# Perceiver layer on one core: three rounded query products, three context buffers, one buffer for residual and output, and new engine orders

## The chip, the core and the metric

The kernel runs on one core of a Trainium2 chip. A core has a matrix engine (TensorE, PE in the profile, with PEld for its weight loads), a vector engine (VectorE, DVE), an activation engine (ScalarE, ACT), a general one (GpSimd, POOL) and SyncE (SP), which here only issues DMAs. Each runs its own instructions in order and they meet at semaphores. The time is that of one execution on the device, in microseconds (us). Before the change it is 835.1 us, the median of three runs from 832.51 to 836.73.

## What is computed

The reference is one perceiver layer over 64 sequences of 32 tokens with 256 channels, each with 257 context rows of 192 channels. Cut to what matters:

```python
x = x + cross_attention(layernorm(x), ctx)     # 16 heads of 64; Wq 256x1024, Wkv 192x2048, Wo 1024x256; key mask
x = x + self_attention(layernorm(x))           # 16 heads of 16, over the 32 tokens of a sequence
r = sigmoid(mix(x, mu_r) @ Wr.T)               # mix: mu * x + (1 - mu) * x of the token before
x = x + r * (square(relu(mix(x, mu_k) @ Wk.T)) @ Wv.T)
```

Both attentions normalise again with a layer norm of their own. All is in fp32, inputs and output.

## The kernel before

The 64 sequences are worked in 8 groups of 8 (GB), so a group has 256 tokens (TOK). The keys of the cross attention are never made: the queries of a group are multiplied with the key weights first (jobs K0 to K11, L677 to L713), which gives for each head a row of 192 numbers to multiply with the context itself.

A long stream of named jobs is written out by hand for each engine: one list for the first group, one for the six middle groups, one for the last group (L63 to L128). A job is called by its name; `:3` behind it is the sequence of the group. The names that matter here:

- CT transposes the context of a sequence (TensorE, L746), rounds it to `cT_h` (ScalarE, L1101) and takes the rest to `cT_l` (VectorE, L1365). S0 to S3 are the scores of a sequence, four heads at a time: five products of 258 columns into one bank (L807), mask and maximum (VectorE, L1374), exponential (ScalarE, L1109). R are reciprocals (VectorE), N the normalising on GpSimd (L565), P the transposes of probabilities (L818, copied at L1117), U their rounding (ScalarE, L1128), L their rest (GpSimd, L431), AC ten products with the context (L835 to L841; 512 columns), whose results ScalarE (L1141, L1142) and VectorE (L1387) copy. CU and CL round the context for AC (L1135, L422 and L423).
- For the group that comes next: A0 to A9 (layer norm, VectorE), XT (transposes of the normalised tokens, L638, copied to `xnT` at L1053), Q0 to Q3 (queries, L657, copied to `qT` at L1057) and K0 to K11 (product L712; rounding on ScalarE L1088, L1092; rest on VectorE L1352, L1356). K0 to K3 and K6, K7 are written into two pairs of banks in turn, so K4 waits for the rests of K0 and K1, and so on. The scores of the next group wait for the rest of K9, those of its last four heads for K11.
- For the group that went before, behind its cross attention: OT0, OT1 (values, L875 to L887), WO0, WO1 (output product, L895, added to the residual at L1411), B0 to B9 (layer norm), T2, QT, KT, VR, SC, PT, PV, T4, PJ (self attention), C0 to C9, T3, M0, M1, FR, FK, KA, FV, YO (feed forward; KA on GpSimd L601, FV at L968 and L1502, YO on GpSimd L607, which adds the residual and makes the output `yo`). XB and X1 (GpSimd, L584, L590) add a bias row to the residual.

What stands after `CT:0` at the end of a list belongs to the next group. In the last group's list the closing jobs have a half behind them (`WO.0`, `WO.1`), since nothing is left beside them; Z jobs are products whose result nobody reads (L997).

SyncE (L502 to L516) loads in each group the tokens of the next but one stage (`xn`), the residual `xb` of the group before (which waits until `yo` of the group before that was made), then a context buffer each time that CL has freed one (`cx_in`, four of them, L512), and stores `yo`. The last residual and the last store have the same form.

The queries are made of fp32 operands:

```python
last = pe.matmul(pre[:, i * TOK:(i + 1) * TOK], wq[:, k, (2 * n + i) * P:(2 * n + i + 1) * P],
                 xnT[:, k, :], start=(k == 0), stop=(k == 1))
```

One such product of a 128x128 block with 256 columns is two matmul records in the profile; a product of operands of type fp32r is one record.

Of the kernel before, what the change touches and what calls it, by code (L numbers as in the profile page):

```python
# [1597 lines left out]
```

## Time and profile before

| | |
|---|---|
| median of 3 runs | 835.1 us (832.51 to 836.73) |
| the profiled execution's own time | 835.41 us |
| its span in the profile | 832.8 us |
| period of a middle group | 98.5 us |
| first group | 0 to about 99 us |
| closing part, behind the last AC | about 779 to 832.8 us |
| TensorE busy | 801.4 us, 96% of the span |
| VectorE, ScalarE, GpSimd busy | 72%, 73%, 50% |
| granted TensorE clock | 1.00 but for one stretch in the closing part |

The span is the time from the first instruction of the program to the last, and the execution's own time holds 2.6 us more around it. A timeline row gives start and length in us, engine, line, operation, output<-inputs, shapes and count, and in brackets the idle time before it with what ended it. The length of a matmul record includes the way through the array, so two following ones overlap: what a product costs is the distance of starts. A period is the stretch from the first scores of one group to those of the next.

### The profile page before, as it was taken

To read this page: it belongs to the slowest core of one execution; us is meant where nothing else is said; L and a number is where in the kernel's file an instruction comes from. 1 tells how busy PE (TensorE), PEld (TensorE's weight loads), DVE (VectorE), ACT (ScalarE), POOL (GpSimd) and SP (SyncE) were. 2 spreads that over 40 slices of the span, in tenths; PEclk is the share of its full clock that TensorE was granted. 3 is DMA by queue.
4 is the path that set the end of the run, shared out by engine and by line. 5 is a ranking of instruction groups with operands and counts; after the bars stand their busy time and mean duration, and the time that the engine had idled before them with its cause. 6 is when DMAs were issued, how large, how long until landed. Compare 5 with 4: busy or idle time off the path is not lost.

```text
span 832.8 us, 20494 instructions
## 1 busy us (share of the span) xinstructions
PE 801.4 (96%) x7497; PEld 665.5 (80%) x7497; DVE 599.3 (72%) x1813; ACT 604.6 (73%) x1439; POOL 417.0 (50%) x664
## 2 busy tenths in 40 slices
PE   9999899998999999998999989999999999999976
PEld 8988688885889778896788868887688977978755
DVE  4865857787587966879577886778668794688376
ACT  3998857887678965789568976789667895778333
POOL 1356445762456624665347534566245672487311
PEclk9999999999999999999999999999999999999999
DMA  8411210111101201012101111011010110100000
GB/s 234 140 32 44 55 26 15 39 27 39 27 15 39 65 1 39 2 40 64 27 15 27 26 52 27 14 39 48 18 27 14 39 52 14 28 14 1 27 2 13
DMA packets 49522, 30.51 MB, mean 37 GB/s; under 512 B 22928, under 2 KB 48336, under 8 KB 49424
## 3 DMA queue, kind: packets, MB, share of 16 engines
q1 hardware_dynamic: 48528, 29.12, 12.9%
q8 instruction: 60, 0.98, 0.5%
q14 instruction: 38, 0.31, 0.1%
q10 hardware_dynamic: 896, 0.10, 0.1%
HBM read 26.85 MB, written 2.10 MB: 35 GB/s over the span
## 4 chain that ended last, share of the span: by engine, by line
PE 79%; DVE 16%; issue 3%; ACT 1%; DMA 0%; POOL 0%; POOLq 0%; ACTq 0%
PE score L807 18%; PE probT L818 6%; PE pre L657 6%; PE post L895 6%; DVE qk_t L1356 5%; DVE qk_l L1352 3%; PE aux L746 3%; PE post L904 3%; PE ac_main L835 3%; PE ac_tail L837 3%; PE ac_main L836 3%; PE ac_tail L841 3%; PE ac_main L840 3%; PE post L875 2%; PE post L881 2%
## 5 line engine op out<-in xcount | busy, mean ns | idle before, releaser
L431 POOL TENSOR_TENSOR prT_l<-prT,prT_h 128x512 fp32r<-128x512 f32 x128 | 165.3, 1292 | 187.0 <-ACT prT_h L1128 186.5
L565 POOL TENSOR_SCALAR pr<-pr,rsum,poison 128x257 f32<-128x257 f32 x256 | 149.4, 594 | 134.8 <-DVE rsum L1380 134.8
L1109 ACT ACTIVATE pr<-sm,nmx 128x257 f32<-128x257 f32 x256 | 129.5, 507 | 61.2 <-DVE nmx L1374 58.1
L1374 DVE CUSTOM_DVE_ANT_0 sm<-score,mbias 128x257 f32<-128x257 f32 x256 | 106.8, 420 | 75.3 <-PE score L807 60.6
L807 PE MATMUL score<-cT_h,qk_h 128*128 128x258 f32 x256 | 89.7, 350 | 7.3 <-DVE qk_t L1356 6.0
L1128 ACT ACTIVATE prT_h<-prT 128x512 fp32r<-128x512 f32 x128 | 80.5, 630 | 20.3 <-PE ac_tail L841 19.1
L1117 ACT ACTIVATE prT<-probT 128x512 f32<-128x512 f32 x128 | 75.6, 591 | 6.7 <-PE probT L818 4.7
L818 PE MATMUL probT<-ident,pr 128*128 128x128 f32 x512 | 79.3, 277 | 0.0
L807 PE MATMUL score<-cT_h,qk_t 128*128 128x258 f32 x256 | 72.8, 284 | 0.0
L807 PE MATMUL score<-cT_h,qk_l 128*128 128x258 f32 x256 | 72.5, 283 | 0.0
L807 PE MATMUL score<-cT_l,qk_h 128*128 128x258 f32 x256 | 72.5, 283 | 0.0
L807 PE MATMUL score<-cT_l,qk_t 128*128 128x258 f32 x256 | 72.3, 282 | 0.0
L1387 DVE TENSOR_TENSOR act_<-ac_tail,act_low 64x256 f32<-64x256 f32 x128 | 52.6, 411 | 26.7 <-ACT act_low L1141 25.5
L818 PEld LDWEIGHTS probT<-ident,pr 128*128 128x128 f32 x512 | 58.5, 141 | 16.1 <-issue 11.5
L807 PEld LDWEIGHTS score<-cT_h,qk_h 128*128 128x128 f32 x256 | 48.4, 189 | 15.1 <-DVE qk_t L1356 8.6
L835 PE MATMUL ac_main<-prT_h,c_hl 128*128 128x512 f32 x128 | 55.6, 434 | 3.2 <-ACT prT_h L1128 2.0
L1365 DVE TENSOR_TENSOR cT_l<-aux,cT_h 128x512 fp32r<-128x512 f32 x64 | 44.1, 688 | 12.7 <-ACT cT_h L1101 12.0
L657 PE MATMUL pre<-xnT,wq 128*128 128x256 f32 x224 | 52.9, 379 | 0.0
L895 PE MATMUL post<-wo,qT 128*128 128x256 f32 x224 | 50.6, 379 | 0.0
L837 PE MATMUL ac_tail<-prT_h,c_hl 128*128 128x512 f32 x128 | 50.4, 394 | 0.0
L836 PE MATMUL ac_main<-prT_h,c_hl 128*128 128x512 f32 x128 | 50.2, 392 | 0.0
L840 PE MATMUL ac_main<-prT_l,c_hl 128*128 128x512 f32 x128 | 50.1, 392 | 0.0
(319 smaller groups left out, 2170.2 us busy)
## 6 DMA issues: line engine op xcount, KB each, us to landing
cx_in<-in_ctx_dram SPq DMA_DIRECT2D x64, 192.0 KB, 2.5
cx_in<-in_ctx_dram SPq DMA_DIRECT2D x64, 64.0 KB, 2.3
xn<-in_x_dram SPq DMA_DIRECT2D x8, 256.0 KB, 2.9
xb<-in_x_dram SPq DMA_DIRECT2D x8, 256.0 KB, 3.0
out_dram<-yo SPq DMA_DIRECT2D x7, 256.0 KB, 2.2
wq<-in_L_xattn_Wq_dram SPq DMA_DIRECT2D x2, 512.0 KB, 6.0
wo<-in_L_xattn_Wo_dram SPq DMA_DIRECT2D x1, 1024.0 KB, 8.2
wqkv<-in_L_attn_W_qkv_dram SPq DMA_DIRECT2D x1, 768.0 KB, 8.9
```

What stands on the lines that cost most here:

```text
L431: eng.tensor_tensor(prT_l[:, :, cut], prT[:, :, cut], prT_h[:, :, cut], ALU.subtract).then_inc(prob_lower, 1)
L565: last = pool.tensor_scalar(p, p, rsum[:, j % 2, t:t + 1], poison[:, 0:1], ALU.mult, ALU.mult)
L657: last = pe.matmul(pre[:, i * TOK:(i + 1) * TOK], wq[:, k, (2 * n + i) * P:(2 * n + i + 1) * P], xnT[:, k, :], start=(k == 0), stop=(k == 1))
L807: last = pe.matmul(score[t % 2][:, 0:NK + 1], q[:, j, tile], c, start=(i == 0), stop=(i == len(products) - 1))
L818: last = pe.transpose(probT[:, m * 256 + i * P:m * 256 + (i + 1) * P], pr[j % 2][:, 2 * half + i, m * P:(m + 1) * P], ident[:])
L835: pe.matmul(ac_main[:], c[:, m, UPPER], prT_h[:, m, :], start=(m == 0), stop=False)
L837: pe.matmul(ac_tail[:], c[:, m, TAILS], prT_h[:, m, :], start=(m == 0), stop=False)
L895: last = pe.matmul(bank[:, 0:DM], qT[:, k, w * P:(w + 1) * P], wo[:, k, :], start=(k == 0), stop=(k == NPAIR - 1))
L1109: act.activation(pr[j % 2][:, t, :], sm[:, t % 2, :], ACT.Exp, bias=nmx[:, j % 2, t:t + 1], scale=-1.0, accum_out=ssum[:, j % 2, t:t + 1]) ...
L1117: act.activation(prT[:, :, half * 256:(half + 1) * 256], probT[:].rearrange("p (m c) -> p m c", m=2), ACT.Copy).then_inc(probT_copied, 1)
L1128: act.activation(prT_h[:, :, cut], prT[:, :, cut], ACT.Copy).then_inc(prob_upper, 1)
L1374: dve.tensor_tensor_reduce(sm[:, t % 2, :], score[t % 2][:, 0:NK], mbias[:], DH ** -0.5, BIG, ALU.add, ALU.min, nmx[:, j % 2, t:t + 1]).th ...
```

## The change

- The queries of groups 1 to 7 (Q0 to Q3) are made of three rounded products in place of one in fp32: upper weights by upper tokens, lower weights by upper tokens, upper weights by lower tokens, each for two halves of the channels. The first group's queries stay in fp32 (`first_queries`).
- For it `wq` is split once: ScalarE rounds it to `wq_h` in four pieces (jobs V0 to V3), GpSimd takes the rest to `wq_l` (V0 to V3). The tokens are split in each group: ScalarE rounds `xnT` to `xnT_h` right behind the copy XT, GpSimd makes `xnT_l` (XL).
- The fp32 `wq` moves into the second half of `acm`'s storage, so the first `acm` copy waits for the split.
- The context has three loading buffers instead of four; buffer numbers run through all sequences.
- `xb`, `x1`, `x2` and `yo` are one buffer. The residual of a group is loaded once the output of the group before has been stored; X1 waits for the layer norm B9 that reads x1; YO works in place.
- All orders are new, and the closing part has 20 Z products instead of 17. The second half's closing tiles lie in `acm` instead of `wq`.

The diff, cut (of the order lists two lines each of TensorE's and GpSimd's middle ones):

```diff
-NCTX = 4
+NCTX = 3
 PE_ORDER = (
-    "S0:0 CT:1 S1:0 OT0 CT:2 S2:0 S3:0 OT1 LV0 P0:0 S0:1 S1:1 LV1 WO0 S2:1 P1:0 S3:1 WO1 S0:2 XT CT:3 S1:2 P0:1 S2:2 S3:2 "
+    "S0:0 S1:0 CT:1 OT0 CT:2 S2:0 S3:0 OT1 LV0 P0:0 LV1 S0:1 S1:1 WO0 S2:1 CT:3 P1:0 S3:1 WO1 P0:1 S0:2 AC:0 S1:2 S2:2 T2 "
...
-    "S1:7 S2:7 FR S3:7 P0:6 FK AC:5 P1:6 FV K0 K2 P0:7 AC:6 K4 K6 P1:7 LT K8 AC:7 CT:0 K10").split()
+    "FR S2:7 S3:7 FK P0:6 AC:5 FV K0 P1:6 K2 P0:7 LT K4 P1:7 AC:6 CT:0 K6 K8 AC:7 K10").split()
...
-        wq = sb("wq", [P, 2, NH * DH])
+        wq_h = sb("wq_h", [P, 2, NH * DH], F32R)
+        wq_l = sb("wq_l", [P, 2, NH * DH], F32R)
+        xnT_h = sb("xnT_h", [P, 2, TOK], F32R)
+        xnT_l = sb("xnT_l", [P, 2, TOK], F32R)
-        x2 = x1
+        x2 = xb = yo = x1
+        wq = stage[:, 2048:4096].rearrange("p (k n) -> p k n", k=2)
...
             def load_residual(g):
-                after(sp, y_ready, g)
+                if g == 0:
+                    sp.wait_ge(ffn_full, 1)
+                after(sp, stored, 16 * g)
...
-                    load_ctx(g * GB + j + NCTX, j % NCTX)
+                    load_ctx(g * GB + j + NCTX, (g * GB + j) % NCTX)
...
                 elif base == "X1":
-                    pool.wait_ge(*copied("WO1" if a is None else name.replace("X1", "WO"), g))
+                    pool.wait_ge(ln_ready[3] if a == 1 else ln_ready[1], 1 if a == 1 else g + 1)
...
+            def weights_lower(n):
+                pool.wait_ge(wq_upper, n + 1)
+                cut = slice(n * 256, (n + 1) * 256)
+                pool.tensor_tensor(wq_l[:, :, cut], wq[:, :, cut], wq_h[:, :, cut], ALU.subtract).then_inc(wq_split, 1)
+            def tokens_lower(g):
+                pool.wait_ge(xnT_upper, g)
+                pool.tensor_tensor(xnT_l[:], xnT[:], xnT_h[:], ALU.subtract).then_inc(xnT_split, 1)
...
                     n = int(name[1])
+                    if n == 0:
+                        pe.wait_ge(xnT_split, g)
+                    if g == 1:
+                        pe.wait_ge(wq_split, n + 1)
                     for i in range(2):
-                        for k in range(2):
-                            last = pe.matmul(pre[:, i * TOK:(i + 1) * TOK], wq[:, k, (2 * n + i) * P:(2 * n + i + 1) * P],
-                                             xnT[:, k, :], start=(k == 0), stop=(k == 1))
+                        cols = slice((2 * n + i) * P, (2 * n + i + 1) * P)
+                        products = [(w[:, k, cols], t[:, k, :]) for w, t in ((wq_h, xnT_h), (wq_l, xnT_h), (wq_h, xnT_l)) for k in range(2)]
+                        for m, (w, t) in enumerate(products):
+                            last = pe.matmul(pre[:, i * TOK:(i + 1) * TOK], w, t, start=(m == 0), stop=(m == len(products) - 1))
...
                 if name == "XT":
+                    after(act, xnT_split, g - 1)
...
+                    if g > 0:
+                        last.then_inc(pre_free, 1)
+                        act.wait_ge(pre_free, nth_pre("XT", g))
+                        act.activation(xnT_h[:].rearrange("p k t -> p (k t)"), xnT[:].rearrange("p k t -> p (k t)"), ACT.Copy).then_inc(xnT_upper, 1)
+                        return
...
+            def weights_upper(n):
+                act.wait_ge(pre_full, nth_pre("G1", 0))
+                cut = slice(n * 256, (n + 1) * 256)
+                act.activation(wq_h[:, :, cut], wq[:, :, cut], ACT.Copy).then_inc(wq_upper, 1)
```

Below are three places of the new order, each before and after. Lines are numbered anew in the changed kernel.

First, TensorE where the first query job (Q0) of a middle group stands. Before (L657 is Q0, L638 is T2, L904 is QT):

```order
L841 MATMUL ac_tail<-prT_l,c_hl 128x512
L638 MATMUL post<-ident,hn 128x128 x4
L657 MATMUL pre<-xnT,wq 128x256 x4
L904 MATMUL post<-hT,wqkv 128x256 x4
L807 MATMUL score<-cT_h,qk_h 128x258
```

Now (L682 is Q0):

```order
L832 MATMUL score<-cT_l,qk_t 128x258
L682 MATMUL pre<-xnT_h,wq_h 128x256 x2
L682 MATMUL pre<-xnT_h,wq_l 128x256 x2
L682 MATMUL pre<-xnT_l,wq_h 128x256 x2
L682 MATMUL pre<-xnT_h,wq_h 128x256 x2
L682 MATMUL pre<-xnT_h,wq_l 128x256 x2
L682 MATMUL pre<-xnT_l,wq_h 128x256 x2
L832 MATMUL score<-cT_h,qk_h 128x258
```

Q0's four fp32 products are twelve rounded ones, and it stands between two score jobs; the transposes XT stand shortly before it, behind VR, where there was a longer stretch between XT and Q0.

Second, ScalarE at the end of a period, from the copy P0:7 to the rounding of K8 and K9. Before (L1117 P, L1128 U, L1141 and L1142 AC:6, L1088 and L1092 the roundings of K4 to K9):

```order
L1117 ACTIVATE prT<-probT 128x2x256
L1141 ACTIVATE act_low<-ac_tail 64x512
L1142 ACTIVATE acm<-ac_main 128x16x32
L1088 ACTIVATE qk_h<-score 128x8x2x32 x2
L1128 ACTIVATE prT_h<-prT 128x2x256
L1088 ACTIVATE qk_h<-pre 128x8x2x32
L1117 ACTIVATE prT<-probT 128x2x256
L1088 ACTIVATE qk_h<-post 128x8x2x32
L1128 ACTIVATE prT_h<-prT 128x2x256
L1092 ACTIVATE qk_t<-score 64x8x2x32 x4
```

Now (L1148 P, L1159 U, L1174 and L1175 AC:6, L1119 and L1123 the roundings, L1132 the context copy CT:0):

```order
L1148 ACTIVATE prT<-probT 128x2x256
L1159 ACTIVATE prT_h<-prT 128x2x256
L1123 ACTIVATE qk_t<-post 64x8x2x32 x2
L1119 ACTIVATE qk_h<-score 128x8x2x32 x2
L1148 ACTIVATE prT<-probT 128x2x256
L1159 ACTIVATE prT_h<-prT 128x2x256 x2
L1174 ACTIVATE act_low<-ac_tail 64x512
L1175 ACTIVATE acm<-ac_main 128x16x32
L1119 ACTIVATE qk_h<-pre 128x8x2x32
L1119 ACTIVATE qk_h<-post 128x8x2x32
L1132 ACTIVATE cT_h<-aux 128x2x256
L1123 ACTIVATE qk_t<-score 64x8x2x32 x4
```

The rounding of K3 has moved behind the copy P0:7 and U1:6, both roundings U0:7 and U1:7 stand ahead of AC:6, and CT:0 ahead of K8; K0, K1 and K2 stand ahead of this piece, with P1:6 between K1 and K2, where P1:6 and U1:6 stood ahead of K0 before.

Third, GpSimd where the token rest XL was put in, in a middle group (L570 is N, L434 is L, L553 and L554 are the columns of CT, L624 is XL):

```order
L434 TENSOR_TENSOR prT_l<-prT,prT_h 128x2x256
L553 COPY cT_h<-left_h 128x2
L554 COPY cT_l<-left_l 128x2
L570 TENSOR_SCALAR pr<-pr,rsum,poison 128x257 x2
L578 COPY lastp<-pr 128x4
L624 TENSOR_TENSOR xnT_l<-xnT,xnT_h 128x512
L570 TENSOR_SCALAR pr<-pr,rsum,poison 128x257 x2
L434 TENSOR_TENSOR prT_l<-prT,prT_h 128x2x256 x2
```

XL stands between N1:2 and N0:3. And GpSimd at the end of a period, before (L607 is YO, L584 XB of the period that follows):

```order
L607 TENSOR_TENSOR yo<-sc,x 128x512
L565 TENSOR_SCALAR pr<-pr,rsum,poison 128x257 x2
L573 COPY lastp<-pr 128x4
L431 TENSOR_TENSOR prT_l<-prT,prT_h 128x2x256 x2
L548 COPY cT_h<-left_h 128x2
L549 COPY cT_l<-left_l 128x2
L565 TENSOR_SCALAR pr<-pr,rsum,poison 128x257 x2
L548 COPY cT_h<-left_h 128x2
```

Now (L564 is LX, L611 YO, L589 XB):

```order
L434 TENSOR_TENSOR prT_l<-prT,prT_h 128x2x256
L564 TENSOR_TENSOR lv<-lvc,keep 128x512
L434 TENSOR_TENSOR prT_l<-prT,prT_h 128x2x256
L611 TENSOR_TENSOR x<-sc,x 128x512
L434 TENSOR_TENSOR prT_l<-prT,prT_h 128x2x256
L553 COPY cT_h<-left_h 128x2
L554 COPY cT_l<-left_l 128x2
L589 TENSOR_TENSOR x<-x,bo_row 128x256 x2
L553 COPY cT_h<-left_h 128x2
```

YO stands between L0:7 and L1:7 instead of ahead of N1:7, LX has moved in from the next period's start, and XB is the first of the next period.

## Rows read from the trace of the kernel before

**Rows 1.** The page's engine totals.

```profile
PE 801.4 (96%) x7497; PEld 665.5 (80%) x7497; DVE 599.3 (72%) x1813; ACT 604.6 (73%) x1439; POOL 417.0 (50%) x664
```

**Rows 2.** Busy time by stretch, a period's length from the middle, and the closing part.

```profile
core 0: us, PE busy (x) PEld busy (x) DVE busy (x) ACT busy (x) POOL busy (x), PEclk, DMA share, GB/s
...
494.80:593.00 98.20, 95.68 (x890) 79.39 (x889) 73.24 (x220) 74.40 (x174) 51.82 (x81) 1.00 0.11 31
...
776.00:833.00 57.00, 45.91 (x516) 35.07 (x508) 33.19 (x93) 16.44 (x44) 8.86 (x11) 0.93 0.03 10
```

**Rows 3.** Waits of TensorE: waited for, us in total, times, longest.

```profile
PE score L807 <- DVE qk_t L1356: 6.0, 6, 1.0
PE pre L712 <- DVE qk_t L1356: 3.1, 7, 0.5
PE score L712 <- DVE qk_l L1352: 3.0, 7, 0.6
PE ac_main L835 <- ACT prT_h L1128: 2.0, 6, 0.3
```

**Rows 4.** Timeline of TensorE, end of a period: start, us, instruction, wait.

```profile
476.28 1.89 PE L968 MATMUL post<-wvT,kM 128*128 128x256 f32 x8
...
493.14 0.36 PE L807 MATMUL score<-cT_h,qk_h 128*128 128x258 f32 x1 [1.00 <-DVE qk_t L1356]
```

**Rows 5.** Timeline of VectorE, the same stretch.

```profile
478.21 0.69 DVE L1502 TENSOR_TENSOR sc<-post,sc 128x512 f32<-128x512 f32 x1 [0.20 <-PE post L968]
...
492.35 0.69 DVE L1365 TENSOR_TENSOR cT_l<-aux,cT_h 128x512 fp32r<-128x512 f32 x1
```

**Rows 6.** Timeline of ScalarE, the same stretch.

```profile
479.29 1.08 ACT L1088 ACTIVATE qk_h<-score 128x512 fp32r<-128x512 f32 x2
...
487.83 2.42 ACT L1092 ACTIVATE qk_t<-score 64x512 fp32r<-64x512 f32 x4
```

**Rows 7.** Chain of waits, a middle period: start, us, what.

```profile
460.10 1.20 PE score L807 x10
461.30 1.73 PE pre L657 x8
```

**Rows 8.** Timeline of TensorE, products of 512 columns in rounded form.

```profile
441.82 0.40 PE L837 MATMUL ac_tail<-prT_h,c_hl 128*128 128x512 f32 x1
442.05 0.39 PE L835 MATMUL ac_main<-prT_h,c_hl 128*128 128x512 f32 x1
```

**Rows 9.** Groups of ScalarE by shape: count, busy us, mean ns, idle before.

```profile
L1128 ACT ACTIVATE prT_h<-prT 128x512 fp32r<-128x512 f32 x128 | 80.5, 630 | 20.3 <-PE ac_tail L841 19.1
...
L1053 ACT ACTIVATE xnT<-pre,cols 128x256 f32<-128x256 f32 x16 | 8.1, 553 | 1.8 <-PE pre L638 1.8
```

**Rows 10.** Groups of GpSimd by shape.

```profile
L431 POOL TENSOR_TENSOR prT_l<-prT,prT_h 128x512 fp32r<-128x512 f32 x128 | 165.3, 1292 | 187.0 <-ACT prT_h L1128 186.5
...
L607 POOL TENSOR_TENSOR yo<-sc,x 128x512 f32<-128x512 f32 x7 | 9.2, 1320 | 0.0
```

**Rows 11.** DMA issues: count, KB, us to landing; waits of SyncE.

```profile
cx_in<-in_ctx_dram SPq DMA_DIRECT2D x64, 192.0 KB, 2.5
...
xb<-in_x_dram SPq DMA_DIRECT2D x8, 256.0 KB, 3.0
out_dram<-yo SPq DMA_DIRECT2D x7, 256.0 KB, 2.2
...
SPq L452 <- DVE c_hl L423: 629.3, 57, 24.7
```

**Rows 12.** Timeline of TensorE, closing part, two like products.

```profile
811.95 1.92 PE L944 MATMUL post<-wproj,q2T 128*128 128x256 f32 x4
...
816.69 1.10 PE L944 MATMUL ac_tail<-wproj,q2T 128*128 128x256 f32 x4 [0.81 <-ACT q2T L1207]
```

**Rows 13.** Busy time by stretch, closing part.

```profile
808.00:816.00 8.00, 7.47 (x80) 5.09 (x80) 3.54 (x14) 2.17 (x7) 1.05 (x1) 0.57 0.01 2
```

**Rows 14.** One line of VectorE: ns shortest, median, longest.

```profile
L422 DVE TENSOR_TENSOR c_hl<-cx_in,c_hl x64: 269/287/1035, 24.1 to 775.5; 128x128 fp32r<-128x128 f32 x64
```

More of the change, by code:

```diff
@@ L111 @@
-DVE_LAST = (
[6 rows of a table removed]
-    "C8.0 C9.0 PJ.1 C0.1 C1.1 C2.1 C3.1 C4.1 C5.1 C6.1 C7.1 C8.1 C9.1 M1.0 M1.1 FR.0 FR.1 SG.0 SG.1 FV.0 FV.1").split()
[5 rows of a table added]
+    "Z16 Z17 Z18 Z19 T3.1 FR.0 FK.0 FR.1 FK.1 FV.0 FV.1").split()
+ACT_FIRST = (
[4 rows of a table added]
+    "U1:5 Q3 S2:7 K0 K1 K2 K3 AC:5 K4 P1:6 K5 U0:6 CU:7 K6 S3:7 U1:6 K7 K8 P0:7 K9 U0:7 P1:7 AC:6 U1:7 K10 CT:0 K11 AC:7").split()
+ACT_ORDER = (
[4 rows of a table added]
+    "AC:5 K0 K1 P1:6 K2 P0:7 U1:6 K3 K4 K5 P1:7 U0:7 U1:7 AC:6 K6 K7 CT:0 K8 K9 K10 K11 AC:7").split()
+ACT_LAST = (
[5 rows of a table added]
+    "T4.1 T3.0 M0.0 T3.1 M0.1 FK.0 EZ.0 FK.1 EZ.1").split()
@@ L119 @@
+DVE_FIRST = (
[4 rows of a table added]
+    "AC:6 K9 CT:0 K10 K11 AC:7").split()
+DVE_ORDER = (
[4 rows of a table added]
+    "S3:7 SG0 R0:7 SG1 R1:7 FV AC:5 K0 CL:7 K1 LT K2 K3 K4 K5 AC:6 K6 K7 CT:0 K8 K9 K10 K11 AC:7").split()
+DVE_LAST = (
[6 rows of a table added]
+    "C9.0 PJ.1 C0.1 C1.1 C2.1 C3.1 C4.1 C5.1 C6.1 C7.1 C8.1 C9.1 M1.0 M1.1 FR.0 FR.1 SG.0 FV.0 SG.1 FV.1").split()
 POOL_FIRST = (
-    "CT:1 CT:2 N0:0 N1:0 N0:1 L0:0 L1:0 N1:1 CT:3 L0:1 N0:2 CT:4 N1:2 L1:1 N0:3 L0:2 CT:5 L1:2 N1:3 N0:4 CT:6 L0:3 L1:3 "
-    "N1:4 L0:4 LX L1:4 N0:5 CT:7 N1:5 CT:0 N0:6 L0:5 L1:5 N1:6 N0:7 N1:7 L0:6 L1:6 L0:7 L1:7").split()
+    "V0 CT:1 N0:0 V1 N1:0 CT:2 N0:1 CT:3 L0:0 L1:0 V2 N1:1 V3 L0:1 N0:2 L1:1 N1:2 CT:4 N0:3 CT:5 L0:2 L1:2 N1:3 XL N0:4 "
+    "L0:3 L1:3 N1:4 N0:5 CT:6 L0:4 N1:5 CT:7 LX CT:0 N0:6 L1:4 L0:5 N1:6 N0:7 L1:5 L0:6 L1:6 N1:7 L0:7 L1:7").split()
@@ L140 @@
 LN_LINKS = LN_STAGES - 1
-FOR_PRE = PRE + tuple(f"A{n}" for n in range(LN_STAGES)) + tuple(f"K{n}" for n in range(N_QK))
+FOR_PRE = PRE + ("XL",) + tuple(f"A{n}" for n in range(LN_STAGES)) + tuple(f"K{n}" for n in range(N_QK))
 OF_BATCH = ("CU", "CL", "U0", "U1", "L0", "L1", "CT", "S0", "S1", "S2", "S3", "R0", "R1", "N0", "N1", "P0", "P1", "AC")
@@ L145 @@
 FIRST_FILL = tuple(f"O{n}" for n in range(10))
-ONCE = ("LV0", "LV1", "F0", "F1", "F2", "T0", "LF", "CN", "J0", "J1", "J2", "J3") + PRE_FIRST[1:] + KEYS_FIRST + FIRST_FILL
+ONCE = ("V0", "V1", "V2", "V3", "LV0", "LV1", "F0", "F1", "F2", "T0", "LF", "CN", "J0", "J1", "J2", "J3") + PRE_FIRST[1:] + KEYS_FIRST + FIRST_FILL
 OF_GROUP = ("LX", "LT")
-FILL = tuple(f"Z{n}" for n in range(17))
+FILL = tuple(f"Z{n}" for n in range(20))
 TP = TOK // 2
@@ L264, in perceiver_layer @@
         ffn_in = [x1, hn, hT]
-        left_in = stage[0:NB, 3584:3584 + 256]
-        half_spare = [spare, wq[:].rearrange("p k n -> p (k n)")]
-        kM_half = [t.rearrange("p (c h t) -> p c h t", c=2, h=8) for t in half_spare]
-        p2T_half = [t[:, 0:512].rearrange("p (c q) -> p c q", c=4) for t in half_spare]
-        mixt_half = [t[:, 0:512].rearrange("p (s t) -> p s t", s=4) for t in half_spare]
-        mix_half = [t[:, 1024:1536].rearrange("p (s t) -> p s t", s=4) for t in half_spare]
-        kr_half = [t[:, 512:768].rearrange("p (k t) -> p k t", k=2) for t in half_spare]
-        ka_half = [t[:, 768:1024].rearrange("p (k t) -> p k t", k=2) for t in half_spare]
+        left_in = act_[0:NB].rearrange("p n t -> p (n t)")[:, 0:256]
+        half_spare = [spare.rearrange("p (s t) -> p s t", t=TP), acm[:, :, 0:TP]]
+        kM_half = [t.rearrange("p (c h) t -> p c h t", c=2) for t in half_spare]
+        p2T_half = [t[:, 0:4] for t in half_spare]
+        mixt_half = [t[:, 0:4] for t in half_spare]
+        mix_half = [t[:, 8:12] for t in half_spare]
+        kr_half = [t[:, 4:6] for t in half_spare]
+        ka_half = [t[:, 6:8] for t in half_spare]
         er_half = [sc[:, a].rearrange("p h k -> p (h k)")[:, 0:DM] for a in range(2)]
@@ L299, in perceiver_layer @@
         pre_full, pre_free = sem("pre_full"), sem("pre_free")
+        xnT_upper, xnT_split, wq_upper, wq_split = (sem(n) for n in ("xnT_upper", "xnT_split", "wq_upper", "wq_split"))
         post_full = sem("post_full")
@@ L604, in job @@
                     pool.wait_ge(*copied(name.replace("YO", "FV"), g))
-                    after(pool, stored, 16 * g)
                     if a is None:
@@ L609, in job @@
                         pool.tensor_tensor(yo[:, a, :], er_half[a], x2[:, a, :], ALU.add).then_inc(y_ready, 1)
+            def weights_lower(n):
[5 more added lines that the diff above has]
+                pool.tensor_tensor(xnT_l[:], xnT[:], xnT_h[:], ALU.subtract).then_inc(xnT_split, 1)
             def run():
                 for name, g, j in stream(POOL_STREAM):
-                    if name == "CT":
+                    if name in ONCE and name[0] == "V":
+                        weights_lower(int(name[1]))
+                    elif name == "XL":
+                        tokens_lower(g)
+                    elif name == "CT":
                         columns(g * GB + j, f"CT{j}")
@@ L742, in aux_job @@
                     j = int(name[2])
-                    pe.wait_ge(ctx_loaded[j % NCTX], g * 32 * (GB // NCTX) + 32 * (j // NCTX + 1))
+                    b = g * GB + j
+                    pe.wait_ge(ctx_loaded[b % NCTX], 32 * (b // NCTX + 1))
                     for m in range(2):
@@ L1140, in weighed @@
                 after(act, act_copied, g * GB + j)
+                if g == 0 and j == 0:
+                    act.wait_ge(wq_split, 4)
                 act.activation(act_low[:], ac_tail[64:128], ACT.Copy).then_inc(tail_lower, 1)
@@ L1197, in post_job @@
                     probs = p2T[:, int(name[-1])] if a is None else p2T_half[a]
-                    last = act.activation(probs.rearrange("p c q -> p (c q)"), bank[:], ACT.Copy)
+                    last = act.activation(probs, bank[:].rearrange("p (c q) -> p c q", c=4), ACT.Copy)
                 elif base == "PV":
@@ L1212, in post_job @@
                     mine = kr if a is None else kr_half[a]
-                    last = act.activation(mine.rearrange("p k t -> p (k t)"), bank[:, 0:2 * n_tok], ACT.Relu)
+                    last = act.activation(mine, bank[:, 0:2 * n_tok].rearrange("p (k t) -> p k t", k=2), ACT.Relu)
                 last.then_inc(post_copied["ScalarE"], 1)
@@ L1225, in last_rows @@
                 act.activation(left_h[:].rearrange("p k b -> p (k b)"), rows_in, ACT.Copy).then_inc(left_upper, 1)
+            def weights_upper(n):
+                act.wait_ge(pre_full, nth_pre("G1", 0))
+                cut = slice(n * 256, (n + 1) * 256)
+                act.activation(wq_h[:, :, cut], wq[:, :, cut], ACT.Copy).then_inc(wq_upper, 1)
             def run():
                 for name, g, j in stream(ACT_STREAM):
-                    if name in KEYS_FIRST:
+                    if name in ONCE and name[0] == "V":
+                        weights_upper(int(name[1]))
+                    elif name in KEYS_FIRST:
                         first_key_copy(name)
@@ L1273, in _ @@
             act.wait_ge(ident_made, 2)
-            act.activation(yo[:, 0, 0:2], ident[:, 0:2], ACT.Copy)
+            act.activation(sm[:, 0, 0:2], ident[:, 0:2], ACT.Copy)
             act.wait_ge(ln1_in, 32)
@@ L1408, in post_job @@
                     dve.wait_ge(xb_ready, g + 1)
-                    after(dve, y_ready, g)
                     dve.tensor_tensor(x1[:, w, :], bank[:, 0:DM], xb[:, w, :], ALU.add).then_inc(post_copied["VectorE"], 1)
```

24 lines of the change are left out of this document (8 added, 16 removed), and 74 rows, old and new, of tables (ACT_FIRST, ACT_LAST, ACT_ORDER, DVE_FIRST).

## The prediction

> **What bounds the kernel now.** Read the engine totals first [rows 1]: TensorE is busy for 96% of the span, the others for 50 to 73%. A total can hide a stage with another limit, so the second view is busy time by stretch [rows 2]: a length of one period from the middle has TensorE busy 95.7 of 98.2 us and ScalarE and VectorE at 75%; only the closing part (57 us, TensorE busy 45.9) is something else, a chain of short steps. The third view is the list of TensorE's waits [rows 3]. All four large entries come six or seven times, once a period, and they name the roundings of K and the probabilities beside them. They sum to 14.1 us, some 2 us a period; what else TensorE waits for in the middle is a few tenths. So the middle is TensorE at work, with one stall at each period's end. In the timelines of that place TensorE starts FV at 476.28 and the next group's scores at 493.14, 16.86 us later, behind a wait [rows 4], while VectorE runs from the start of FV's product at 478.21 to the end of the context's rest at 493.04 [rows 5], 14.83 us, and I find no hole above 0.1 us between. There VectorE is the bound. ScalarE's run from the rounding of K0 at 479.29 to the end of K9's at 490.25 is 10.96 us [rows 6], over two us ahead of VectorE's end.
>
> **The rounded queries.** A fp32 query job costs 1.73 us in the chain of waits [rows 7], eight records in one piece. Its replacement has 12 products of 256 columns. The same chain shows ten rounded products of 258 columns in 1.20 us [rows 7], 0.120 each, and products of 512 columns start 0.23 apart [rows 8]; the nearest shape is the first, with two columns more. So a job becomes 12 x 0.120 = 1.44 us and saves 0.29. Groups 1 to 7 have four jobs each, 28 in all: 28 x 0.29 = 8.1 us of TensorE, and nearly all of them stand in stretches where TensorE is the bound. If the two columns less gave nothing and some entry cost of 0.05 a job came on top, 6.7; a larger gain than 28 x (1.73 - 12 x 0.115) = 9.8 has no row. I take 8.1.
>
> On this the Trainium skill ("TensorE: Matmul & The Clock Gate", Back-to-back issue gap) gives for a product behind another N/2.4 + 2.5 ns for N columns. By that page 256 columns would be 109 ns, a job 1.31 us, and the gain 28 x 0.42 = 11.8 us. The trace does not agree: it has 230 ns at 512 columns where that rule gives 216, and 120 at 258 where it gives 110 [rows 7, 8]. The measured distance decides, and the sum stays at 8.1.
>
> **What splitting costs.** Per group ScalarE gets a rounding of 128x512 (0.63 us by its twin on the probabilities [rows 9]) and GpSimd a difference of the same shape (1.29 [rows 10]); once, four of each for the weights, 2.5 and 5.2 us. In the middle ScalarE is idle for 24 of 98 us and GpSimd for 46 [rows 2], which hides it so long as nobody waits for the result. Who waits is Q0. From XT's end: two copies of 0.55 that overlap to 1.0, the rounding 0.63, the difference 1.29, and some 0.3 of handing over, 3.3 us, with XT's own 0.4 3.7. Between XT and Q0 TensorE now has AC:1 (ten products at 0.23, 2.3), a context transpose 0.4, SC0 1.0, P1:2 0.4 and a score job 0.6: 4.7 us. One us of cover remains, so I cost it at nothing. If GpSimd is held in N1:2 ahead of XL, the cover is gone, and behind the waiting Q0 stand all scores: bounds 0 and 1.1 us (one N job) a group. In the first group the four weight roundings stand between exponentials; both bounds are 0 and 2.5 us, I take 0.6 together with other small waits.
>
> **Three context buffers.** SyncE waits for CL nearly all the time [rows 11], so a load leaves as soon as its buffer is free and lands 2.5 us later, 3.4 with its two issues. The tightest new pair is CL:4 and CT:7: T4, AC:3, PJ, P1:4, S0:6 and S1:6 lie between on TensorE, 0.4 + 2.3 + 1.7 + 0.4 + 1.2 = 6.0 us. In the first group the sixteen small loads of the last rows now stand ahead of the load of context 5, but about 15 us of TensorE's work lies between their start and CT:5, against some 10.6 for the issues and 3.4. Cost nothing; if late, 1 to 2 us, once.
>
> **One buffer for residual and output.** The residual's load now follows YO (1.32 [rows 10]), the store's landing (2.2) and its own (3.0 [rows 11]), then XB: about 9 us from YO's start, with N0:0 of the next group behind XB on GpSimd. YO starts some 6 us ahead of the period's end, XB is done 3 us into the new one, and P0:0 is wanted 11 us into it. Nothing, with 6 us in reserve.
>
> **The end of a period.** The new order has the same VectorE work between FV and the next scores, so the 14.83 us stay [rows 5]. ScalarE gets three jobs into its run from K0 to K9 that stood outside: P1:6, U1:6 and the context copy CT:0, at 0.5 to 0.6 each as they follow one another there. Its run becomes 10.96 + 1.6 = 12.5. K0's product stands directly behind FV (1.74 + 1.1), so ScalarE starts 3.0 us after FV's start and ends at 15.5. VectorE's last pair begins with its half K8 ready at 14.3, at its turn, and its own 2.8 us end at 17.1; the scores start at 17.2 instead of 16.86. In exchange TensorE has P1:6 (0.44) within this stretch, which stood ahead of FV before. Net -0.1 us a period, so zero: the stall of 2 us stays. Bounds: the list's 14.1 us all gone [rows 3], or ScalarE the bound (rival one).
>
> **T2 and the closing part.** T2 stands 4.5 us behind WO1 instead of 6; the layer norm B between them takes about that long packed as it now is on VectorE: 0.1 to 0.2 a group, +0.6 in all, within the 0.6 above. In the closing part the clock was granted at 0.57 over 808 to 816 us [rows 13], a mix of the two levels, 1.2 and 2.4 GHz; before that TensorE had a hole of nearly two us around 806. PJ.0 took 1.92 us there against 1.10 for PJ.1 behind it [rows 12]. The new order fills more (three Z behind SC.1, two behind VR.0), places T2.0 ahead of WO.1 and PJ.0 ahead of PT.1, and lets YO.0 start ahead of the second reciprocal. If the dip goes and the order helps, -2.5; if not, +0.5. I take -1.0.
>
> **Sum.** The profiled execution took 835.41 us, 0.3 above the median. 835.41 - 8.1 + 0.6 - 1.0 = 826.9 us; I say 827.
>
> A rule that speaks against the change is one on GpSimd's port. The trace shows a VectorE difference of two SBUF tiles at 287 ns median and 1035 at most [rows 14]. The Trainium skill ("SBUF — State Buffer", Who interferes with whom) says that a VectorE instruction with two SBUF inputs and a GpSimd one that reads SBUF exclude each other for a whole instruction; the long record agrees. By it the seven XL could add up to 7 x 1.29 = 9 us to VectorE; where XL stands VectorE has idle time, and at the period's end its inputs are mostly PSUM, so the sum is the same with the rule and without.
>
> **Rivals.**
> - ScalarE becomes the bound at each period's end (slower). For: it gets 1.6 us more there, and the copy of Q3 now stands right ahead of FK, on the way to FV, 0.5 more. Against: it was over two us ahead. It decides once K9's rounding ends more than 1.4 us behind VectorE's turn for K8. Price 7 x 2.1 = 14.7 over the forecast: 841.7 us. Chance 0.07.
> - The new waits eat the gain (no change). For: XL, T2, FV and the buffers all have covers of only 1 to 3 us. Price: one N job a period, 7 x 1.1 = 7.7: 834.6. Chance 0.18.
> - The new orders take out part of the stall too. For: 14.1 us are there to be had, and the roundings of K are mixed otherwise with AC:6 and P. Against: VectorE has no hole there to close. Half gone: 827 - 7 = 820. Chance 0.15.
> - The forecast, 822 to 831: chance 0.60.
>
> **From cases to numbers.** About 0.5%, 4.2 us, is what a measurement of this kernel can tell from no change: faster is below 830.9, slower above 839.3. Faster takes the third rival, nearly all of the forecast's case and little of the second: 0.74. Same 0.19, slower 0.07. The range reaches from below the third rival to just past the second, 819 to 835, and leaves out the slow case and the far end of the third rival.
>
> **What would show it.** Right: a query job as one piece of 1.4 to 1.45 us with products 0.12 apart; a period of 97.4 instead of 98.5; no wait of TensorE for the token rest; the list of TensorE's waits still some 14 us and naming the K roundings. Wrong: a wait of Q0 for GpSimd, of the scores for ScalarE's rounding of K8 and K9, of a context transpose for a landing, or a period that shrinks by much more than 1.15 us, for then the order did it. The closing part (from its last AC to the end) tells apart the two halves of the sum: it was 54 us.

## The result: 830.1 us against 834.6, half of the gain that was forecast

| | before | changed |
|---|---|---|
| median | 834.63 us (14 runs, 832.51 to 836.73) | 830.11 us (14 runs, 829.37 to 831.97) |
| ratio to before | | 0.9954, 95% interval 0.9945 to 0.9963 |
| span in the profile | 832.8 us | 827.9 us |
| first group ends (its successor's OT0) | 101.55 us | 102.33 us |
| period | 98.42 us | 97.45 us |
| OT0 of the last group to the end | 140.7 us | 140.8 us |
| of that, behind the last AC | 53.6 us | 53.2 us |

The change is faster by 4.5 us by the medians (3.8 by the ratio) where 8.1 were forecast, inside the range. The page's totals after, which answer to [rows 1]: TensorE has lost only 3.8 us of busy time.

```profile
PE 797.6 (96%) x7615; PEld 664.9 (80%) x7615; DVE 599.0 (72%) x1813; ACT 611.7 (74%) x1450; POOL 427.4 (52%) x675
```

Busy time by stretch, a period and the closing part (start and end, length, then busy time and instructions of each engine, clock), for [rows 2]:

```profile
492.14:589.62 97.48, 95.30 (x905) 79.47 (x906) 73.12 (x220) 75.03 (x175) 52.34 (x82) 1.00 0.12 31
770.00:827.86 57.86, 46.89 (x538) 36.54 (x534) 34.39 (x93) 18.18 (x48) 10.22 (x12) 0.94 0.04 15
```

The chain of waits where Q0 and Q1 stand, for [rows 7]: each is one piece of 1.42 us, twelve products 0.118 apart, as the sum had it.

```profile
435.22 1.42 PE pre L682 x12
436.64 1.21 PE score L832 x10
437.85 1.42 PE pre L682 x12
```

TensorE's waits, for [rows 3]. No query job waits for the rest of the tokens. The roundings of K are still the largest entry, but all the waits for them sum to 9.3 us where they were 12.1. The second entry is OT0 of each group, 0.4 us, for which the view names no other engine; before it was 0.3 a group, 1.7 in all.

```profile
PE score L832 <- DVE qk_t L1397: 6.5, 6, 1.1
PE post L900 <- issue: 2.5, 6, 0.4
PE score L736 <- DVE qk_l L1393: 2.5, 7, 1.1
...
PE ac_main L860 <- ACT prT_h L1159: 1.3, 2, 0.8
```

The period's end, TensorE, for [rows 4]: from FV to the next scores it is now 17.51 us (16.86 before), 0.44 of which is P1:6.

```profile
472.29 1.89 PE L993 MATMUL post<-wvT,kM 128*128 128x256 f32 x8
...
489.80 0.39 PE L832 MATMUL score<-cT_h,qk_h 128*128 128x258 f32 x1 [1.09 <-DVE qk_t L1397]
```

VectorE there, for [rows 5]: it has four small holes, each for ScalarE, the first at 475.87 and the others in the last six us, with packed work between.

```profile
475.87 0.69 DVE L1393 TENSOR_TENSOR qk_l<-score,qk_h 128x512 fp32r<-128x512 f32 x1 [0.21 <-ACT qk_h L1119]
...
483.78 0.85 DVE L1428 TENSOR_TENSOR act_<-ac_tail,act_low 64x256 f32<-64x256 f32 x2 [0.19 <-ACT act_low L1174]
484.89 0.69 DVE L1393 TENSOR_TENSOR qk_l<-pre,qk_h 128x512 fp32r<-128x512 f32 x1 [0.26 <-ACT qk_h L1119]
...
486.93 2.81 DVE L1397 TENSOR_TENSOR qk_t<-score,qk_t 64x512 fp32r<-64x512 f32 x4 [0.16 <-ACT qk_t L1123]
```

ScalarE there, for [rows 6]: from the rounding of K0 to the end of K9's it runs 475.23 to 488.12, 12.9 us without a hole; it was 10.96, and 12.5 were forecast.

```profile
475.23 1.08 ACT L1119 ACTIVATE qk_h<-score 128x512 fp32r<-128x512 f32 x2 [0.40 <-PE score L736]
...
485.22 0.62 ACT L1132 ACTIVATE cT_h<-aux 128x512 fp32r<-128x512 f32 x1
485.70 2.42 ACT L1123 ACTIVATE qk_t<-score 64x512 fp32r<-64x512 f32 x4
```

The rest of the tokens on GpSimd ends at 433.45; Q0 starts at 435.06, so 1.6 us of cover were left.

```profile
432.17 1.28 POOL L624 TENSOR_TENSOR xnT_l<-xnT,xnT_h 128x512 fp32r<-128x512 f32 x1
```

In the closing part the clock still dips, for [rows 12] and [rows 13]: behind a stretch where TensorE was busy 2.31 of 4 us it is granted 0.63, a mix of 1.2 and 2.4 GHz. PJ.0 now stands ahead of that, at 805.81, and takes 1.10 us (1.92 before); the dip falls on PJ.1, which takes 2.01 (1.10 before).

```profile
807.00:811.00 4.00, 2.31 (x41) 1.56 (x39) 2.68 (x12) 1.61 (x4) 0.00 (x0) 0.95 0.00 0
811.00:815.00 4.00, 4.00 (x14) 3.21 (x13) 2.14 (x10) 1.10 (x4) 0.00 (x0) 0.63 0.00 0
```

```profile
810.53 2.01 PE L969 MATMUL ac_tail<-wproj,q2T 128*128 128x256 f32 x4 [0.81 <-ACT q2T L1240]
```

The dip is shorter than before: over these 8 us the clock was low for about 3.4, worked out from 0.95 and 0.63, where 0.57 over 808 to 816 gives 6.9. And it isn't in every execution. Experiment 9 has the same closing part; in its profile the clock stays at 1.00 there, and PJ.1 takes 1.10 us:

```profile
811.00:815.00 4.00, 3.78 (x18) 2.96 (x18) 2.65 (x13) 1.66 (x5) 0.00 (x0) 1.00 0.00 0
```

From the end of the last AC (779.26 before, 774.67 now) to the end, the closing part takes 53.6 us before, 53.2 now with the dip, and 52.15 in experiment 9 without it.

So what is missing is not in the query jobs' own time. The first group, whose queries alone should have saved 1.2, grew by 0.8; each period shrank by 0.97 and not by 1.16; the last group and the closing part together stood still where -1.0 was forecast, because the last group grew by 0.5 up to its last AC and the closing part shrank by 0.4.

### The profile page after: what moved, and what is told of

It is laid out like the page before. It is cut to its first block, busy times and chain, and to the rows that moved or that the text cites. A ratio compares the mean times of both kernels' runs of the same rounds, so it can differ in the third digit from the quotient of the medians.

```text
span 827.9 us, 20761 instructions
## 1 busy us (share of the span) xinstructions
PE 797.6 (96%) x7615; PEld 664.9 (80%) x7615; DVE 599.0 (72%) x1813; ACT 611.7 (74%) x1450; POOL 427.4 (52%) x675
## 3 DMA queue, kind: packets, MB, share of 16 engines
q1 hardware_dynamic: 48528, 29.12, 12.9%
## 4 chain that ended last, share of the span: by engine, by line
PE 82%; ACT 7%; DVE 6%; issue 3%; DMA 1%; POOLq 0%; POOL 0%; SPq 0%; ACTq 0%; DVEq 0%
PE score L832 17%; PE probT L843 6%; PE post L920 6%; PE pre L682 5%; PE ac_main L860 3%; PE ac_tail L862 3%; PE aux L771 3%; PE ac_main L861 3%; PE ac_tail L866 3%; PE ac_main L865 3%; PE post L929 3%; DVE qk_t L1397 2%; PE post L900 2%; PE post L948 2%; PE post L906 2%
## 5 line engine op out<-in xcount | busy, mean ns | idle before, releaser
L434 POOL TENSOR_TENSOR prT_l<-prT,prT_h 128x512 fp32r<-128x512 f32 x128 | 169.6, 1328 | 144.4 <-ACT prT_h L1159 143.9
L570 POOL TENSOR_SCALAR pr<-pr,rsum,poison 128x257 f32<-128x257 f32 x256 | 146.8, 584 | 115.2 <-DVE rsum L1421 115.2
L832 PE MATMUL score<-cT_h,qk_h 128*128 128x258 f32 x256 | 87.3, 341 | 6.8 <-DVE qk_t L1397 6.5
L1148 ACT ACTIVATE prT<-probT 128x512 f32<-128x512 f32 x128 | 76.0, 594 | 13.6 <-PE probT L843 11.2
L1159 ACT ACTIVATE prT_h<-prT 128x512 fp32r<-128x512 f32 x128 | 79.2, 624 | 8.4 <-PE ac_tail L866 7.2
L866 PE MATMUL ac_tail<-prT_l,c_hl 128*128 128x512 f32 x128 | 50.1, 391 | 0.0
```

What stands on the lines that cost most here:

```text
L434: eng.tensor_tensor(prT_l[:, :, cut], prT[:, :, cut], prT_h[:, :, cut], ALU.subtract).then_inc(prob_lower, 1)
L570: last = pool.tensor_scalar(p, p, rsum[:, j % 2, t:t + 1], poison[:, 0:1], ALU.mult, ALU.mult)
L832: last = pe.matmul(score[t % 2][:, 0:NK + 1], q[:, j, tile], c, start=(i == 0), stop=(i == len(products) - 1))
L1148: act.activation(prT[:, :, half * 256:(half + 1) * 256], probT[:].rearrange("p (m c) -> p m c", m=2), ACT.Copy).then_inc(probT_copied, 1)
L1159: act.activation(prT_h[:, :, cut], prT[:, :, cut], ACT.Copy).then_inc(prob_upper, 1)
```

## Experiments

Medians, and ratios to runs of the kernel before on the same chip (834.5 to 834.7 us).

**1. The queries back in fp32** (`e1_fp32_queries`): new orders and buffers stay.

```diff
-products = [... for w, t in ((wq_h, xnT_h), (wq_l, xnT_h), (wq_h, xnT_l)) for k in range(2)]
+products = [... for w, t in ((wq, xnT),) for k in range(2)]
-V0 V1 V2 V3 XL      (all lists), and the rounding behind XT
```

> The changed kernel with its new orders and buffers, but the queries of groups 1 to 7 made of fp32 products again; the rounding of weights and tokens and their rests are left out. Theory A (the rounded job is worth what the distance of starts says, 1.725 - 1.418 = 0.307 us a job, 28 jobs = 8.6 us, and the splitting in the first group costs up to 1.7 us): 837.0 to 838.7 us, and the period grows from 97.45 to about 98.7. Rival B (a fp32 job that stands ahead of a rounded product takes only 1.54, so the rounded one is worth 0.12 there): 833.5 us, period 97.9.

Measured: 837.39 us, 1.0032 [1.0019, 1.0044], slower than before. The period is 98.57 to 98.93 us, 98.67 on average. Against the changed kernel that is 7.3 us by the medians, 6.5 by the ratios; 28 jobs at 0.23 to 0.26 us. The traces show more: 1.1 to 1.2 us a period, 0.28 to 0.31 a job. Theory A holds, and with it the distance of starts: at the same place a fp32 job is 1.73 in the chain.

```profile
440.62 1.73 PE pre L677 x8
442.35 1.22 PE score L827 x10
443.56 1.73 PE pre L677 x8
```

A timeline alone misleads here: the job starts at 440.46 and the next product at 442.00, 1.54 later, but that product then holds TensorE for 0.30 instead of 0.12.

```profile
440.46 1.89 PE L677 MATMUL pre<-xnT,wq 128*128 128x256 f32 x8
442.00 0.47 PE L827 MATMUL score<-cT_h,qk_h 128*128 128x258 f32 x1
442.30 0.29 PE L827 MATMUL score<-cT_l,qk_h 128*128 128x258 f32 x1
```

What remains of the change, orders and buffers, costs 2.7 us by the medians; by the traces 2.45 in the first group and 0.15 to 0.25 a period.

**2. The old orders with rounded queries** (`e2_old_orders`) **and 3. with fp32 queries** (`e3_buffers_only`), both with the new buffers.

```diff
-PE_ORDER = ("S0:0 S1:0 CT:1 OT0 CT:2 ...      (the new lists, all engines)
+PE_ORDER = ("S0:0 CT:1 S1:0 OT0 CT:2 ...      (the old lists; e2 with V0 to V3 and XL put in)
+CL:1 ahead of CT:4, CL:2 of CT:5, CL:3 of CT:6, CL:4 of CT:7
```

> The changed kernel with rounded queries and new buffers, but the old orders on all engines (V0 to V3 and XL put in, and CL:1 to CL:4 moved ahead in places, as three buffers need). Theory A (the rounded queries bring 8.6 us and the new orders take about 4 back): 826 to 828 us, period about 97.2, the stretch from FV to the next scores 16.9 us. Rival B (what is missing is lost to the splitting itself, its roundings and rests and the waits for them): 830 us, period 97.4 or more.

> Old orders and fp32 queries with the new buffers only: three context buffers, one buffer for residual and output (CL:1 to CL:4 moved ahead in places). Theory A (the buffers cost nothing): 834.6, within 0.6 us. Rival B (late loads or the residual's return cost 1 us or more a period): 837 us or more, with TensorE's waits naming a DMA.

Measured: 903.91 us and 869.51 us, 1.0831 and 1.0418. In experiment 2 neither theory holds. In experiment 3 Theory A falls and Rival B holds, at many times the price it named: the new buffers are not free in the old order. The waits of TensorE there name transfers, which they never do before. The period is 100.3; the first group (to 114.05) and the stretch from OT0 of the last group (152.1) are longer by 12.5 and 11.3 us:

```profile
PE aux L767 <- DMA cx_in<-in_ctx_dram: 24.9, 10, 8.1
```

and in experiment 2 the first query job as well, whose cover in my sum was "one us". Here it is gone: Q0 waits up to 4.6 us a group, and the period is 105.9:

```profile
PE aux L775 <- DMA cx_in<-in_ctx_dram: 25.1, 11, 8.2
...
PE pre L686 <- POOL xnT_l L628: 27.6, 6, 4.6
```

XL stood behind N1:1 on GpSimd there; N waits for reciprocals, for up to 12.8 us. So these two say how narrow the covers are, and nothing on how the loss of 2.7 is shared.

**4. Without the rest of the tokens** (`e4_no_token_rest`): the third pair of products reads the rounded tokens, so a part of the queries isn't computed.

```diff
-for w, t in ((wq_h, xnT_h), (wq_l, xnT_h), (wq_h, xnT_l))
+for w, t in ((wq_h, xnT_h), (wq_l, xnT_h), (wq_h, xnT_h))
-XL      (GpSimd's lists)
```

> The changed kernel without XL, GpSimd's rest of the tokens: the third pair of products reads the rounded tokens again, so that part of the queries isn't computed. Theory A (XL is hidden and disturbs nothing): 830.1, within 0.5 us. Rival B (XL delays GpSimd's jobs behind it or VectorE beside it): 827 to 829 us, the gain spread evenly over the seven groups.

Measured: 830.33 us, 0.9948 [0.9932, 0.9964]. Theory A: XL costs nothing, to VectorE neither, which is busy for 598.8 us without it and 599.0 with it.

**5. The new orders alone, in the kernel before** (`e5_new_orders_only`).

```diff
-PE_ORDER = ("S0:0 CT:1 S1:0 OT0 CT:2 ...
+PE_ORDER = ("S0:0 S1:0 CT:1 OT0 CT:2 ...      (all lists, without V and XL; NCTX = 4, xb, x1 and yo apart)
```

> The kernel before with the new orders alone (20 Z products with them): fp32 queries, four context buffers, residual and output apart. With the changed kernel but for its queries at 837.4 us and before at 834.7, theory A (the orders are what costs 2.7 us, the buffers nothing): 837.4, within 0.7, the first group 2.4 us longer than before and each period 0.2. Rival B (three context buffers and the shared buffer cost it): 834.7 or less, first group as before.

Measured: 844.27 us, 1.0114 [1.0100, 1.0127]. Neither theory holds: the orders alone cost 9.7 us, and the new buffers give 6.9 of it back. The first group ends at 103.43, 1.9 later than before. The period is 99.44 us in most groups, and TensorE has a wait that is 0.3 us in all in the kernels before and of experiment 1, T2 for the layer norm B:

```profile
PE post L641 <- DVE hn L1311: 6.1, 8, 1.0
```

The reason is on GpSimd. With its own buffer X1 waits only for WO1, and runs beside B:

```profile
424.08 1.44 POOL L593 TENSOR_TENSOR xb<-x,bp_row 128x256 f32<-128x256 f32 x2
```

```profile
424.26 0.59 DVE L1308 TENSOR_SCALAR lw<-lw 128x2 int32<-128x2 int32 x1
424.89 0.78 DVE L1318 SCALAR_TENSOR_TENSOR lw<-lw 128x1 f32<-128x1 f32 x2
...
426.68 0.74 DVE L1311 TENSOR_SCALAR hn<-x,mv,lw 128x256 f32<-128x256 f32 x2
```

In experiment 1, same orders but one buffer, X1 must wait until B has read it; then the same steps take 0.17 and 0.35, and `hn` is ready 0.85 us sooner after WO1.

```profile
422.29 0.17 DVE L1333 TENSOR_SCALAR lw<-lw 128x2 int32<-128x2 int32 x1
422.50 0.35 DVE L1343 SCALAR_TENSOR_TENSOR lw<-lw 128x1 f32<-128x1 f32 x2
...
423.85 0.74 DVE L1336 TENSOR_SCALAR hn<-x,mv,lw 128x256 f32<-128x256 f32 x2
```

In the kernel before X1 waits for WO1 too, but its place in the old order is far behind B, whose `hn` is ready at 422.01:

```profile
427.53 1.41 POOL L590 TENSOR_TENSOR xb<-x,bp_row 128x256 f32<-128x256 f32 x2
```

Six periods at 0.85 are 5.1 of the 6.9 us. No run changes X1's wait alone, and four loading buffers against three differ as well; that the wait is the cause is read from these rows. What is behind the 1.9 us of the first group stays open: from 8 us on TensorE is idle for 0.6 us more of it, the rest is busy time.

**6. The old period end** (`e6_old_period_end`), in the first and the middle groups, and **7. the same in the middle groups alone** (`e12_old_end_middle`).

```diff
-... AC:5 FV K0 P1:6 K2 P0:7 LT K4 P1:7 AC:6 CT:0 K6 K8 AC:7 K10
+... AC:5 P1:6 FV K0 K2 P0:7 AC:6 K4 K6 P1:7 LT K8 AC:7 CT:0 K10      (and its like on ScalarE and VectorE)
```

> The changed kernel with the old order of TensorE, ScalarE and VectorE from FV (in the first group from K0) to the end of the period. Theory A (the new period end costs 0.2 us a period, 0.65 longer from FV to the next scores against 0.44 for P1:6 in it): 828.4 to 829.2 us, FV to scores 16.9 us, period 97.25. Rival B (the period end is bound by the same VectorE work either way and P1:6 fits in for nothing): 830.1 or more, period 97.45.

> The changed kernel with the old order from FV to the end of the period in the six middle groups alone. Its window was 16.95 us where it also stood in the first group, and the period 97.38 against 97.45. Theory A (both period ends cost the same once P1:6 is counted, within 0.1 us a period): 829.6 to 830.3 us. Rival B (the new end costs the 0.2 a period that the window alone says): 828.8 or less.

Measured: 834.06 us for the first; its first group ends at 106.08, so the old end doesn't fit behind the new first group. In its middle: window (from FV to the next scores) 16.95, period 97.40. The second: 829.12 us, 0.9936 [0.9923, 0.9949], a little below the changed kernel, with intervals that overlap; period 97.40. So the new end costs 0.05 us a period by the traces and up to 0.17 by the medians, between the two theories: the window alone shows 0.12 once P1:6 (0.44) is counted, and this comes back partly outside it.

**8. CL:7 taken off VectorE, new end** (`e7_rest7_gpsimd`, first and middle groups) and **9. old end** (`e9_end_and_rest7`, middle groups).

```diff
-CL:7      (VectorE's lists)
+L1:6 CL:7 ...      (GpSimd's)
```

> The changed kernel with one job taken off VectorE at each period's end: the rest CL:7 of the context is made by GpSimd, behind L1:6. Theory A (VectorE's run from FV to K9 is what bounds the period's end, 0.6 us of it are CL:7): 0.5 us less a period, seven of them, 826 to 827.5 us, the stall ahead of the scores 0.5 smaller. Rival B (ScalarE, or the products of the K jobs, bound it as closely): 829.5 to 830.5. Rival C (GpSimd gets late with the rests of the probabilities): over 831, with TensorE waiting for L:7.

> As the kernel with the old period end in the six middle groups, and there the rest CL:7 of the context is made by GpSimd behind L1:6. Theory A (with the old end VectorE's run bounds the window, with the new one ScalarE's, which is why taking CL:7 off VectorE did nothing there): window 16.3 us in place of 16.95, period 96.8, 825.8 to 827 us. Rival B (VectorE is not the bound in the old end either): window 16.95, period 97.4, 829.6 to 830.5 us.

Measured: 832.43 us, 0.9974 [0.9962, 0.9986], and 829.47 us, 0.9948 [0.9936, 0.9961]. With the new end the window stays at 17.52: VectorE has a hole where CL:7 was, and from K4 on runs as before, at ScalarE's pace.

```profile
381.27 1.70 DVE L1440 TENSOR_TENSOR spread<-aux,seqm 32x256 f32<-32x256 f32 x4 [0.57 <-PE aux L780]
...
390.49 2.81 DVE L1401 TENSOR_TENSOR qk_t<-score,qk_t 64x512 fp32r<-64x512 f32 x4 [0.16 <-ACT qk_t L1127]
```

With the old end the window shrinks by 0.16, and OT0 starts 0.15 later behind it; the period stays at 97.4. There the context CT:0 holds the scores next, and ScalarE's copies of AC:7 hold OT0:

```profile
488.21 0.60 ACT L1136 ACTIVATE cT_h<-aux 128x512 fp32r<-128x512 f32 x1 [1.30 <-PE aux L775]
```

```profile
488.91 0.69 DVE L1410 TENSOR_TENSOR cT_l<-aux,cT_h 128x512 fp32r<-128x512 f32 x1
```

```profile
PE post L904 <- ACT acm L1179: 3.8, 6, 0.6
```

So Theory A of both falls: 0.69 us of VectorE's work taken away is worth nothing in either order. Experiment 8 is 2.3 us slower than the changed kernel, a time that Rival C named, but TensorE has no wait for L:7. The difference lies in the first group (to 103.22) and in the time around the span (3.4 to 3.7 us in five of its six runs, where the changed kernel mostly has 2.1); the periods are equal. Why is open.

**10. The old closing order** (`e8_old_closing`).

```diff
-AC:7 WO.0 OT0.1 OT1.1 T2.0 Z0 WO.1 Z1 QT.0 ...      (20 Z)
+AC:7 WO.0 OT0.1 OT1.1 Z0 WO.1 T2.0 QT.0 ...      (17 Z)
```

> The changed kernel with the old order behind the last AC on TensorE, ScalarE and VectorE, and 17 Z products instead of 20. Theory A (the new closing order is worth 0.4 us): 830.5. Rival B (it is worth the 1.0 that was forecast, or 2.5): 831.1 to 832.6. The clock of TensorE dips somewhere in the closing part in every case.

Measured: 830.62 us, 0.9949 [0.9935, 0.9963], as Theory A said, but with intervals that overlap: the new closing order is worth 0.5 us or nothing by the times. The profile shows where a gain would come from. Behind the last AC it has 53.9 us against 53.2, with the clock at 0.76, 0.50 and 0.89 over 803 to 815, so low for about twice as long. That the clock dips in every case, as I had expected, doesn't hold: in the profile of experiment 9 TensorE's work in the closing part meets no dip.

**11. The old first group** (`e10_old_first`) and **12. all three edits** (`e11_all_three`).

```diff
-PE_FIRST, ACT_FIRST, DVE_FIRST, POOL_FIRST      (new)
+                                                 (old, with V0 to V3, XL, and CL:1 to CL:3 ahead)
-if g == 0 and j == 1: spread_last_values()
+if g == 0 and j == 2: spread_last_values()
```

> The changed kernel with the old orders in the first group alone (V0 to V3 and XL put in, the rests CL:1 to CL:3 moved ahead, as three buffers need, and the sixteen small loads of the last rows behind the load of context 5 instead of 4). Theory A (the new order of the first group loses some 2 us, and the splitting of the weights nothing): 828 us, the first group ends at 100.3 instead of 102.3. Rival B (three buffers and the weights' splitting are what costs there, whatever the order): 830 to 832 us, first group 102.3 or more.

> The last three edits together: old first group, old period end, CL:7 on GpSimd in the middle groups. If the terms add: 830.1 - 2 - 3.8 = 824.3 us. If neither theory holds: 830 us or above.

Measured: 834.33 us, 1.0004 [0.9995, 1.0012], first group to 107.18; and 834.01 us, so the terms don't add. Theory A falls for this version of the old order. In its first 105 us GpSimd sits behind V for 11.6 us, TensorE waits 2.8 for normalised probabilities and 1.8 for a context:

```profile
POOL wq_l L622 <- ACT wq_h L1267: 11.6, 2, 10.8
```

```profile
PE probT L846 <- POOL pr L573: 2.8, 3, 1.5
PE aux L774 <- DMA cx_in<-in_ctx_dram: 1.8, 1, 1.8
```

Whether it is the place of V or of CL:1 to CL:3 that costs most here was not tested apart. That the new first group loses 1.9 us even without any splitting is shown by experiment 5; a better one was not found.

## Why the prediction was right, and where its terms were off

Against before: forecast -8.1 for the queries and -0.4 for everything else; measured, by the medians, -7.3 and +2.7. So the mechanism of the gain was right, and what went wrong is in the terms that were put at nothing or nearly so. That the period came out as forecast, 97.45 for 97.4, is in part luck: the queries give 1.1 to 1.2 us of it, and orders and buffers take 0.15 to 0.25 back.

- **The query jobs**: right. 0.118 a product and 1.42 a job, where 0.120 and 1.44 were taken from the chain [rows 7]. The gain of 11.8 us that followed from the Trainium skill ("TensorE: Matmul & The Clock Gate", Back-to-back issue gap) doesn't come out here: 0.118 against the 0.109 that the page gives as the gap of an isolated product. Taking the 1.54 that a timeline shows would have given 0.12 a job, which experiment 1 refutes. Worth 7.3 us of 8.1 by the medians (6.5 by the ratios), and 7.8 to 8.5 by the periods of the traces, so whether anything is missing here is not shown.
- **The splitting at nothing**: right, by experiment 4 and by the first group of experiment 1: with its fp32 queries but without V it is 1.7 us longer, of which the four query jobs are 1.2. The cover was 1.6 us, and when it is gone (experiment 2) the wait is four times what the second rival named, 4.6 us a group for 1.1.
- **Buffers at nothing**: the step that failed in kind. I costed only the transfers, which are on time in the new order but for one wait of 0.3 us. But I did not cost the wait that the shared buffer puts in front of X1. In the new orders that wait is worth up to 6.9 us if the rows of experiment 5 are read rightly, because it keeps GpSimd out of B's way; I had written that T2 waits 0.1 to 0.2 longer, with B "packed as it now is". That held only thanks to this wait.
- **The period's end**: forecast 17.2 and a net of nothing; 17.51, and 0.05 to 0.17 a period. I read VectorE's run without a hole [rows 5] as the bound. Experiment 9 shows that in the old end it leads the chain AC:7, CT:0 by 0.16 us at most. In the new end VectorE waits for ScalarE, whose run ends 15.8 us after FV's start where 15.5 were forecast, and experiment 8 shows that less work on VectorE doesn't help: the mechanism of the first rival, with 0.3 us on the window for its 2.1. Of the third rival, half of the stall gone, there is a small part: TensorE's waits for the roundings of K fell from 12.1 to 9.3 us, with P1:6 filling part of them. Whether an order exists that shortens all these chains no run shows.
- **The first group**: 0.6 was taken for all small waits; the new order costs 1.9 there before any splitting. I looked for the cost of what is added and did not compare the order's own waits. By the trace this is the largest mis-sized term: the queries should have taken 1.2 from this group, and it grew by 0.8.
- **The closing part**: -1.0 taken; -0.4 by the trace behind the last AC, 0 to -0.5 by experiment 10. The dip is shorter and, in several executions, gone; then it is -1.4 where I had put -2.5. Part of the whole gain hangs on this: among all executions with a mean granted clock of 0.998 or more the median span is 830.8 us before (7 of 50) and 827.7 now (8 of 14), 3.1 apart; among the others it is 832.8 and 828.2, 4.6 apart.

By place, in the two profiles: 5.0 us were gained where the sum had 8.5. The first group is short by 2.0, less the 0.6 that the sum had for small waits; the six periods by 1.1; the last group and the closing part by 1.1. Of the periods' part the new end is 0.3 to 1.0, and OT0's longer wait 0.8 in all; these runs don't settle their shares.
